# Attention scores on half the rows of the array: two heads as 62-row float32r matmuls, and the causal mask of the maxima added on TensorE

## The reference

```python
xn = _layernorm(x)
qkv = clip(xn @ Wqkv.T, -8, 8); q, k, v = split(qkv)           # 512 each
q, k = layer_norm(q)*w+b, layer_norm(k)*w+b                    # over all 512, then 32 heads of 16
scores = q.k * 16**-0.5 + slope[head] * (kpos - qpos)          # ALiBi
scores = where(kpos <= qpos, scores, -1e30)
s = (softmax(scores) @ v) @ Wout.T
g = silu((silu(xn @ gate) * (xn @ up)) @ down)                 # int4 weights, 512 -> 1792 -> 512
out = x + s * g
```

## Time and profile before

| | us |
|---|---|
| median of 3 runs (lowest, highest) | 1147.9 (1145.27, 1156.36) |
| profiled execution: its own time | 1146.97 |
| its span, first to last instruction | 1145.1 |
| PE busy | 1077.1 |
| DVE busy | 876.7 |
| ACT busy | 663.8 |
| POOL busy | 368.6 |

### The profile page before, as it was taken

How to read it: one execution, slowest core, us unless ns; L and a number is a source line. 1 busy time by engine, 2 the same in 40 slices (tenths; PEclk the granted TensorE clock), 3 DMA queues, 4 the chain that set the end, 5 groups by cost and what they waited for, 6 DMA issues and landing times. The chain is left out here.

```text
span 1145.1 us, 18720 instructions
## 1 busy us (share of the span) xinstructions
PE 1077.1 (94%) x6401; PEld 676.6 (59%) x6401; DVE 876.7 (77%) x2083; ACT 663.8 (58%) x1061; POOL 368.6 (32%) x474
## 2 busy tenths in 40 slices
PE   5999988999999999999999998999999999999997
PEld 4788764433333333333333333788888888887885
DVE  6788897888887887888788782677867876777776
ACT  3666556666666676676767667544544454445443
POOL 2666635121211221121122112133424433343343
PEclk9999999999999999999999999999999999999999
DMA  6255753453445436343444512100110020012001
GB/s 209 77 154 154 200 131 124 123 134 87 114 105 155 106 93 143 84 133 83 144 107 118 125 51 87 37 1 10 58 45 1 19 93 1 1 37 74 1 1 38
DMA packets 99663, 98.95 MB, mean 86 GB/s; under 512 B 28144, under 2 KB 81008, under 8 KB 99568
## 3 DMA queue, kind: packets, MB, share of 16 engines
q1 hardware_dynamic: 97936, 97.36, 31.1%
q10 hardware_dynamic: 1632, 0.39, 0.2%
HBM read 76.09 MB, written 21.23 MB: 85 GB/s over the span
## 5 line engine op out<-in xcount | busy, mean ns | idle before, releaser
L893 ACT ACTIVATE pr<-pair 128x1024 f32<-128x1024 f32 (+3 forms) x384 | 293.2, 811 | 151.5 <-PE pair L1010 97.0
L268 DVE CUSTOM_DVE_ANT_0 bank<-bank,sg 128x384 f32<-128x384 f32 (+1 forms) x488 | 227.6, 522 | 65.7 <-PE bank L278 62.7
L1270 DVE SCALAR_TENSOR_TENSOR gate<-pair,sgu,gate 128x512 f32<-128x512 f32 x168 | 126.1, 751 | 94.9 <-PE pair L1349 94.9
L1348 PE MATMUL pair<-xc_lo,w_gu 128*128 128x512 f32 x448 | 175.6, 392 | 1.5 <-DVE xc_lo L1253 1.5
L1349 PE MATMUL pair<-xc_hi,w_gu 128*128 128x512 f32 x448 | 174.7, 390 | 0.0
L271 DVE TENSOR_REDUCE mx<-bank 128x1 f32<-128x512 f32 x240 | 150.2, 683 | 8.9 <-PE bank L278 8.2
L1140 POOL TENSOR_TENSOR h_lo<-gate,h_hi 128x512 fp32r<-128x512 f32 x56 | 72.5, 1294 | 241.8 <-ACT h_hi L1165 241.8
L1190 ACT ACTIVATE gate<-gate 128x512 f32<-128x512 f32 x56 | 35.5, 634 | 168.5 <-DVE gate L1270 168.5
L278 PE MATMUL bank<-ks,qs 108*128 108x512 bf16 (+3 forms) x384 | 107.7, 329 | 5.4 <-DVE mx L268 5.1
L278 PE MATMUL bank<-xin_c,s_sb 108*128 108x512 bf16 (+3 forms) x344 | 97.5, 332 | 4.6 <-DVE mx L268 4.3
L1005 PE MATMUL pair<-s_sb,xin_c 111*128 111x512 bf16 (+3 forms) x384 | 94.4, 330 | 7.8 <-ACT dt L396 2.9
(11 more groups left out here) (116 smaller groups left out, 1955.5 us busy)
## 6 DMA issues: line engine op xcount, KB each, us to landing
stk<-parts SPq DMA_DIRECT2D x16, 768.0 KB, 5.6
zst<-in_z_all SPq DMA_DIRECT2D x24, 448.0 KB, 4.2
xin_c<-in_x SPq DMA_DIRECT2D x32, 256.0 KB, 3.0
sst<-in_w_all SPq DMA_DIRECT2D x16, 448.0 KB, 6.0
s_sb<-stk SPq DMA_DIRECT2D x96, 64.0 KB
xin_c<-stk SPq DMA_DIRECT2D x96, 64.0 KB
qs<-stk SPq DMA_DIRECT2D x96, 64.0 KB
ks<-stk SPq DMA_DIRECT2D x96, 64.0 KB
```

Source lines behind the costliest of these rows:

```text
L268: dve.tensor_tensor_reduce(out=src, in0=src, in1=tri[:, 512 - w:512], scale=1.0, scalar=-3.0e38, op0=ALU.add, op1=ALU.max, accum_out=dst). ...
L893: act.activation(pr[e % 3][:, 2 * p:2 * p + 2, 0:w], pair[p][:, :, 0:w], ACT.Exp, scale=SCALE)\
L1270: dve.scalar_tensor_tensor(out=a, in0=GB[j % 4], scalar=scale_of(n, k, it), in1=a, op0=ALU.mult, op1=ALU.add)\
L1348: pe.matmul(GB[j % 4], w, xc_lo[:, k, :], start=True, stop=False)
```

## The change

1. q and k are split in **two float32r parts** (`high` on ACT, `low` on POOL). `residual` and `mid` are gone. `stk` is float32 with two parts.
2. The stacked operands have 3 blocks of 16 rows, 12 bias rows and 2 rows for the maximum: 62 rows, float32r. Heads 0 and 2 of a group lie on partitions 0 to 61, heads 1 and 3 on partitions 64 to 125. A score matmul so uses an array shape of 64 rows x 128 columns, at row 0 or row 64, and the two of a pair of heads are issued one behind the other, into different banks.
3. The bias rows come as bfloat16 and have to be float32 in DRAM: POOL casts them in 8 pieces in tiles 0 to 3 of phase A (`cast_row`), through one buffer `row32`, and SP stores each (`store_row`); each cast waits until the store before has landed.
4. In phase B, the mask of the 32 diagonal pieces of the maxima is added by a 128-column bfloat16 matmul of the full shape per piece, so that DVE always uses TENSOR_REDUCE. In phase A DVE still masks.
5. `chain` has 3 instructions instead of 5; `send_d` issues two DMAs instead of one; `spread` places two pieces at a time.

```diff
-ROWS_MAX = 108
-ROWS = 111
+PARTS = 3 * HD
+BIAS = 12
+ROWS_MAX = PARTS + BIAS
+ROWS = ROWS_MAX + 2
...
+            for h in range(2):
+                r0 = 64 * h
+                for r, both in enumerate(((0, 0), (0, 1), (1, 0))):
+                    rows = slice(r0 + r * HD, r0 + (r + 1) * HD)
+                    for a, dst in enumerate((qs[s][rows, b, :, :], ks[s][rows, :, cols])):
+                        src = stk[a, i // GROUPS, p0:p0 + 64, g // 2, both[a], cols]
...
-                while at < len(lot) and (h == hi - 1 or sum(pc[3] + 60 for pc in lot[:at]) < work * passed / total):
-                    out[h].append(lot[at])
-                    at += 1
+                while at < len(lot) and (h == hi - 1 or sum(pc[3] + 110 for pc in lot[:at]) < work * passed / total):
+                    out[h] += lot[at:at + 2]
+                    at += 2
...
-        def score(pe, s, pc, b, n, banks=3):
+        def score(pe, s, pc, b, n, banks=3, full=True):
 
             qt, j, k0, w = pc
-            if not (isinstance(n, int) and n < banks):
+            rows = slice(64 * (j % 2), 64 * (j % 2) + ROWS_MAX)
+            if n >= banks:
                 pe.wait_ge(m_free, n - banks + 1)
-            pe.matmul(b[:, 0:w], qs[s][0:ROWS_MAX, qt // 4, j, (qt % 4) * P:(qt % 4 + 1) * P],
-                      ks[s][0:ROWS_MAX, j, k0:k0 + w], start=True, stop=True).then_inc(m_full, 1)
+            mm = pe.matmul(b[:, 0:w], qs[s][rows, qt // 4, j // 2, (qt % 4) * P:(qt % 4 + 1) * P],
+                           ks[s][rows, j // 2, k0:k0 + w], start=True, stop=full)
+            if full:
+                mm.then_inc(m_full, 1)
...
+        def cast_row(pool, n):
+
+            rows = GROUPS * (BIAS + (3 if n >= GH else 0))
+            pool.wait_ge(row_in, 32)
+            if n > 0:
+                pool.wait_ge(row_out, 16 * n)
+            pool.tensor_copy(row32[0:rows, :], row16[n // GH][0:rows, n % GH, :]).then_inc(row_cast, 1)
...
+                        elif x in LATE[HEAD:] or not last:
+                            score(pe, s if x in LATE[HEAD:] else 1 - s, x, ring_bank(x, last), base(i) + at(x, last),
+                                  full=not on_diagonal(x))
+                            if on_diagonal(x) and x[1] % 2:
+
+                                for head in (x[1] - 1, x[1]):
+                                    pe.matmul(ring_bank((x[0], head, x[2], x[3]), last)[:, x[3] - P:x[3]], behind[:, :], identb[:, :],
+                                              start=False, stop=True).then_inc(m_full, 1)
...
-                        j = 2 * p + jj
-                        mm = pe.matmul(pair[p][:, jj, 0:512 - c0], ks[s][0:ROWS, j, kt * P:(kt + 1) * P],
-                                       qs[s][0:ROWS, qb, j, c0:512], start=True, stop=not diag[e])
+                        rows = slice(64 * jj, 64 * jj + ROWS)
+                        mm = pe.matmul(pair[p][:, jj, 0:512 - c0], ks[s][rows, p, kt * P:(kt + 1) * P],
+                                       qs[s][rows, qb, p, c0:512], start=True, stop=not diag[e])
```

More of the change, by code:

```diff
@@ L137, in build @@
             sst = sbb("sst", [P, HALF], F32)
-            qs.append(sbb("qs1", [P, 2, GH, 512], BF16))
-            ks.append(sbb("ks1", [P, GH, SEQ], BF16))
+            with ExitStack() as c3:
+                row16 = [sb_in(c3)(f"row16{n}", [P, GH, SEQ], BF16) for n in range(2)]
+            qs.append(sbb("qs1", [P, 2, 2, 512], F32R))
+            ks.append(sbb("ks1", [P, 2, SEQ], F32R))
             vs.append(sbb("vs1", [P, QT, GH * VW], F32))
@@ L142, in build @@
             dneg = sbb("dneg", [P, 16], F32)
-            dres = sbb("dres", [P, 16], F32)
-            d3 = sbb("d3", [P, 3, 16], BF16)
-            dt_sb = [sbb(f"dt{n}", [48, P], BF16) for n in range(2)]
+            d2 = sbb("d2", [P, 2, 2, 2, 4], F32R)
+            dt_sb = sbb("dt", [32, P], F32)
             rec = sbb("rec", [P, 2, 4, GH], F32)
@@ L175, in load @@
             cols = slice(b * 512, (b + 1) * 512)
[L176 to L187, removed]
+            g, p0 = i % GROUPS, (i % 2) * 64
+            for h in range(2):
[4 more added lines that the diff above has]
+                        src = stk[a, i // GROUPS, p0:p0 + 64, g // 2, both[a], cols]
+                        sp.dma_start(dst.bitcast(F32), src.rearrange("(n h c) s -> h c n s", n=2, h=2)[h]).then_inc(stk_in[s][b], 16)
+                sp.dma_start(qs[s][r0 + PARTS:r0 + ROWS_MAX, b, :, :].bitcast(F32),
+                             q32[g, :, :, cols].rearrange("r (n h) s -> h r n s", h=2)[h]).then_inc(stk_in[s][b], 16)
+                sp.dma_start(ks[s][r0 + PARTS:r0 + ROWS, :, cols].bitcast(F32),
+                             k32[g, 0:BIAS + 2, :, cols].rearrange("r (n h) s -> h r n s", h=2)[h]).then_inc(stk_in[s][b], 16)
             if b == 0 and values:
@@ L225, in spread @@
             width = [w for e in range(NSTEP) for w in (512 - STEPS[e][2], 512 - STEPS[e][2], 512 - STEPS[e - 1][2])]
-            total, work = sum(width[lo:hi]), sum(pc[3] + 60 for pc in lot)
+            total, work = sum(width[lo:hi]), sum(pc[3] + 110 for pc in lot)
             out, at, passed = {h: [] for h in range(PLACES)}, 0, 0
@@ L258, in base, with on_diagonal, take @@
             return PREP + RING * i
-        def take(dve, pc, b, n):
+        def on_diagonal(pc):
+            return pc[2] + pc[3] == (pc[0] + 1) * P
+        def take(dve, pc, b, n, mask=True):
             qt, j, k0, w = pc
@@ L265, in take @@
             dve.wait_ge(m_full, n + 1)
-            if k0 + w == (qt + 1) * P:
+            if mask and on_diagonal(pc):
                 dve.tensor_tensor_reduce(out=src, in0=src, in1=tri[:, 512 - w:512], scale=1.0,
@@ L473, in _ @@
                         clip_v(pool, t)
+                    for n in row_parts(t):
+                        cast_row(pool, n)
                     for kt in wo_parts(t):
@@ L567, in _ @@
                 send_d1(act, 0, 1, 1, b_xt)
-                mid(t - 2, 1)
                 affine(t - 1, 1)
@@ L670, in _ @@
                     maxima(t, 1)
-                    if t > 0:
-                        residual(dve, t - 1, 0)
                 t = TILES - 1
@@ L683, in _ @@
                 maxima(t, 3)
-                residual(dve, t - 1, 1)
                 maxima(t, 4)
@@ L966, in _ @@
                 dve.memset(b_o[:, :], 0.0).then_inc(o_clear, 1)
-                for a in range(2):
-                    residual(dve, TILES - 1, a)
                 def body(i, s, ip, last):
```

119 lines of the change are left out of this document (53 added, 66 removed).

## The result

| | before | changed |
|---|---|---|
| median us (lowest, highest) | 1149.88 (1145.27, 1156.36) | 1364.45 (1360.08, 1369.82) |
| ratio (95% interval) | | 1.186 (1.178 to 1.194) |
| span of the profiled execution | 1145.1 | 1368.0 |
| first copy of transposed maxima (end of phase A) | 185.9 | 218.6 |
| from there to the last such copy (15 groups) | 497.0 | 679.9 |

1205 us was forecast, 1108 to 1258 the range. The 15 groups took 183 us more, phase A 33 more; after the last such copy the two are level within some 8 us. A copy of transposed maxima (`dt` on ACT) comes once per group and is used as the group's mark throughout. An execution that comes out over 1.5% above the fastest of its kernel, at a lower granted clock, is left out of the ratios.

The account below looks back on a forecast made before the run. PE was taken to bound phase B, 29.1 of 32 us per group. The terms summed to +3.4 us per group, +53 us over 15.5 groups, and +5 in phase A: 1146.97 + 53 + 5 = 1205 us, range 1108 to 1258.

Parts of the forecast that it names:

- What bounds phase B: Phase B: PE is the bound, 29.1 of 32 us per group; the rest short waits, longest in sum on DVE's reduction.
- Scores, -7.0 us: Phase B, per group: both scores of a pair run at the same time on array halves, 15.6 to 8.6 us.
- shape +5.6: Phase B, per group: changes of array shape go from 27 to 83, 56 more at 0.10 us each.
- weights +3.3: Phase B, per group: float32r weight loads stand 0.09 us more uncovered at each of 36 stretches of half-shape scores.
- the forecast 3.4: Phase B: net loss per group, the sum -7.0 + 1.8 + 5.6 + 3.3 + 0.4 - 0.7 us.
- the one set at zero: Phase B: DVE gets a diagonal pair's first piece some 0.5 us later, while still having one to work on; priced zero.
- ACT, +0.4 us: Phase B, per group: `send_d` issues twice; the second issue costs up to 0.6 us per send, mostly off the path.
- The clock: Phase B: the prediction's sum has no term for a change of the granted clock.
- Phase A, +5 us: Phase A: bias-row casts waiting for stores cost 9 us, between 0 and 24; tiles 11 to 15 gain 4.
- 'Free changes': Rival: changes to the half-row shape cost nothing, DVE becomes the bound, 1106 us; chance 0.22.
- 'Weights hidden': Rival: shape changes cost, but weight loads go ahead and waits shrink, some 1152 us; chance 0.15.
- 'No concurrency': Rival: the halves don't work at the same time, or float32r matmuls are slow, about 1340 us; chance 0.13.

Follow-up runs that it names:

- 12: Changed kernel, with the first maxima score of a pair in phase B waiting until both banks are free: 1349 us, ratio 1.173.
- 4: Changed kernel with every score in the full array shape, one after the other, masks, order and float32r as changed: 1265 us, ratio 1.101.
- 6: Changed kernel with every mask also added in the half shape, two matmuls of 64 rows instead of one of 128: 1236 us, ratio 1.073.
- 8: Changed kernel with float32 bias rows without casts, maxima masked on VectorE again, and second-pass masks in the half shape: 1204 us, ratio 1.046.
- 3: Kernel before, with the maxima's scores contracting over rows 0 to 63 only, in bfloat16, one after the other: 1196 us, ratio 1.041.
- 7: Changed kernel with both heads of a pair computed on the lower half of the rows, hence one after the other: 1762 us, ratio 1.530.
- 5: Changed kernel with bias rows given in float32 and copied DRAM to DRAM by two DMAs, no casts: 1327 us, ratio 1.152.
- 10: Kernel before, in bfloat16, with both passes' scores on half rows, odd heads on the upper half: 1160 us, ratio 1.008.
- 9: Kernel before, in bfloat16, with both passes' scores over rows 0 to 63 only, always the lower half: two runs, 1234 and 1308 us.

## Why the prediction was wrong, point by point

**What bounds phase B**: that TensorE leads was right for the kernel before. In the changed kernel it was right only in part, since the forecast left out that the two engines hold each other up (12).

**Scores, -7.0 us, shape +5.6, weights +3.3.** The mechanisms held one by one: pairs side by side, 0.10 us per change between half rows and full (I had it for 32 and 64 columns only), 0.11 us per uncovered float32r load where 0.09 was taken. By the Trainium skill (TensorEngine Tiling, Key Properties) a change of mode drains whatever the shape; runs and trace agree, at 0.10 us. Without these two, a pair that doesn't wait takes 0.22, 0.16 and 0.11 us for 512, 384 and 256 columns, as summed.

**Where the group of 39.0 us goes beyond 36.3**, which is 32.9 and the forecast 3.4. Summed from start to start over the group at 533.3 us and one of before at 319.7 us: second pass 8.1 against 7.9 us, its masks 3.4 against 2.1, maxima 12.5 against 11.6, their masks 3.7 against 0, `pv` 9.2 and 9.3. The term that was mis-sized is the one set at zero without a row behind it: DVE getting its piece late. In 10 of the 16 diagonal pairs, and in 4 of the other 8, the second score starts 0.15 to 0.53 us behind the first, held by its bank until VectorE has read it; so it doesn't run beside the first, and VectorE waits for both masks. These delays are 4.4 us in the group, and the maxima take 12.5 us where pairs by themselves take 8.5 (12). Experiment 12 shows that it can't be had back by waiting earlier. The 2.7 us per group above the sum, some 40 us in all, are what is left over and not a measured price; and a group of 4 loses about as much as this one without any half rows.

**ACT, +0.4 us.** The second DMA issue was seen, but its price was put on ACT, and no wait of PE on the landing was in the sum: the maxima landed 1.5 us late in every other group. How much of this is the second issue isn't shown; 4, 6 and 8 issue twice as well and have hardly such a wait.

**The clock, not in the sum at all.** This is the step that failed most: every term was priced at 2.4 GHz, because the rows of before show 1.00. The change replaced streams on 108 to 111 rows by shorter ones with gaps, added a standstill, and the granted clock fell to 1.2 GHz for 231 of 680 us. With the standstill's 11 us, it cost 15 x (45.3 - 39.0) = 95 us; the run of experiment 4, at full clock, is 92 us shorter beyond its shorter group. The Trainium skill (TensorE: Matmul & The Clock Gate, A second HAM failure mode: psum-queue depth-cycling) tells of a kernel whose clock goes up and down because TensorE idles for short times between groups of matmuls. The changed kernel has such gaps and such a clock, and agrees so far, but 3 has 603 more gaps than before and stays near 1.00. That section doesn't say what 7 shows, that idle rows count.

**Phase A, +5 us**, measured 33. The mechanism was named and its range reached to 24; the size was off. Six of the eight stores landed 3.0 to 3.6 us after their issue, as forecast, but two took 9.2 and 8.5. SP had issued the 1 MB of `raw_out`, which itself took 9.2 us, just ahead of the one, and parts of q and k for `stk` ahead of the other; that they came late for this reason is a reading, no run moved them apart. TensorE, held up so, fell to half clock for 34 us in phase A, 3 without the casts (5). The 5.5 us that are left without them are not explained by a run.

**The rivals.** None hit. 'Free changes' is refuted by 3. 'Weights hidden' by the pair's stretch in 10 against the changed kernel's. 'No concurrency' came nearest in time (1340), but by luck: the halves do work at the same time. The 216 us of phase A and the 15 groups split into 33, 95 with the clock, and 15 x 5.9 = 88 for groups of 39.0 against a mean of 33.1, where the forecast had 5, nothing and 15 x 3.4 = 51.

Open is what exactly lets the clock fall in groups without a standstill; and no version tried was faster than the kernel before.

## What to carry to other kernels

Before giving a matmul fewer rows or a tile shape of its own, count how often the order alternates between shapes: each change cost 0.10 us here, and in float32r 0.11 more for the weight load, together as much as the stream of a 512-column matmul. Ask too whether the engine that reads the results keeps pace with two at once. Price a thinner TensorE at both of its clocks: a kernel at 1.00 that is given shorter streams, idle rows and one more wait of 1.5 us lost as much by the clock here as by all the instructions of its groups. A buffer that is refilled through DRAM costs the landing of its store, and here that was 3 us for six stores and 9 for the two that stood behind a large one.

## What the runs showed of the hardware that was not expected

The granted clock did not follow the busy share alone, but also how many rows of the array work at a time: scores on one half of the rows in float32r (7) gave 0.52 over 470 us with PE written down as busy 467 of them, against 0.84 with as many matmuls in the same order on both halves. It takes more than idle rows now and then: with the maxima alone on one half (3) the clock stayed near 1.00. The same bfloat16 group took 35.7 us or 59 us in one execution (the longer one of 9), by the clock alone. A wait of 1.5 to 1.7 us was followed in six of seven cases by 24 to 27 us at half clock.
